# Projection pieces of 64 rows among the score tiles, and scores two units ahead, in an attention and expert kernel

## What is computed

```python
x = x + layernorm(attention(layernorm(x)))      # 16 heads of 16, biases on q, k, v and out
x = x + layernorm(experts(layernorm(x)))        # 16 experts of width 128, the best 8 mixed, and a shared one

# attention, per batch of 1024 tokens and per head:
scores = q @ k.T                                # q scaled by 1/4
attn = softmax(scores, axis=-1)
ctx = attn @ v
```

## Time and profile before

| | |
|---|---|
| median of 3 runs | 2850.79 us (2848.54 to 2851.70) |
| the profiled execution | 2851.26 us |
| its span, first to last instruction | 2849.5 us |
| mean granted clock of TensorE | 0.987 |
| PE busy | 96% of the span |
| DVE / ACT / POOL busy | 77% / 57% / 36% |
| attention stage, first to last product | 105.3 to 1644 us |

### The profile page before, as it was taken

The page is one execution under the profiler, slowest core; times in us unless marked ns, Lnnn a source line. Parts: engine busy times, 40 slices in busy tenths (PEclk is TensorE's granted clock), DMA queues, the critical chain, the costliest instruction groups (busy, mean ns, idle before and its releaser), DMA issues.

```text
span 2849.5 us, 47674 instructions
## 1 busy us (share of the span) xinstructions
PE 2738.6 (96%) x16514; PEld 1683.1 (59%) x16514; DVE 2207.1 (77%) x4585; ACT 1638.4 (57%) x3159; POOL 1039.5 (36%) x1057
## 2 busy tenths in 40 slices
PE   4999999999999999999999899999999999999997
PEld 2434333343343343433433388888888888888886
DVE  4898998999988989989899667666666666666654
ACT  1477777777777777877778843333333333333332
POOL 4042562654544635636545545111111111111112
PEclk8899999999999999999999999999999999999999
DMA  5303422343234144333332323222222222232221
GB/s 88 55 27 57 65 60 54 63 83 58 53 63 63 42 65 64 64 59 63 63 67 66 88 78 105 82 78 77 74 82 83 79 79 71 82 82 79 79 73 54
DMA packets 136640, 197.33 MB, mean 69 GB/s; under 512 B 22336, under 2 KB 84816, under 8 KB 134352
## 3 DMA queue, kind: packets, MB, share of 16 engines
q1 hardware_dynamic: 136400, 194.29, 31.0%
HBM read 108.74 MB, written 17.30 MB: 44 GB/s over the span
## 4 chain that ended last, share of the span: by engine, by line
PE 83%; SPq 7%; ACT 4%; DVE 3%; issue 2%; POOL 1%; DMA 1%; POOLq 0%; ACTq 0%; DVEq 0%
PE o_bank L558 15%; PE y_bank L681 13%; PE g_bank L667 13%; PE u_bank L667 13%; PE sm_bank L548 13%; PE st_bank L536 7%; SPq L340 4%; PE job_bank L582 4%; ACT probs L933 3%; PE job_bank L591 2%; DVE score_max L1044 1%; PE job_bank L603 1%; SPq L365 1%; SPq L364 1%; SPq L344 1%
## 5 line engine op out<-in xcount | busy, mean ns | idle before, releaser
L1044 DVE TENSOR_REDUCE score_max<-sm_bank 128x1 f32<-128x512 f32 x2048 | 1299.6, 681 | 140.7 <-PE sm_bank L548 136.5
L933 ACT ACTIVATE probs<-st_bank 128x512 f32<-128x512 f32 x2023 | 1080.5, 599 | 313.6 <-PE st_bank L536 310.7
L548 PE MATMUL sm_bank<-qk_stack 64*128 64x512 f32 x2048 | 794.2, 462 | 15.9 <-DMA qk_stack<-qk_stack 11.2
L536 PE MATMUL st_bank<-qk_stack 64*128 64x512 f32 x2023 | 750.0, 451 | 40.4 <-ACT probs L933 31.5
L548 PEld LDWEIGHTS sm_bank<-qk_stack 64*128 64x128 f32 x2048 | 331.6, 188 | 558.1 <-DVE score_max L1044 509.8
L558 PE MATMUL o_bank<-probs,v_quad 128*32 128x512 f32 x4096 | 547.9, 607 | 9.1 <-ACT o_sb L841 7.0
L1191 DVE TENSOR_TENSOR h<-gate_act,u_bank 128x512 f32<-128x512 f32 x256 | 176.2, 688 | 313.1 <-ACT gate_act L895 312.9
L895 ACT ACTIVATE gate_act<-g_bank 128x512 f32<-128x512 f32 x272 | 162.4, 597 | 418.3 <-PE u_bank L667 418.2
L536 PEld LDWEIGHTS st_bank<-qk_stack 64*128 64x128 f32 x2023 | 312.9, 185 | 123.6 <-ACT probs L933 97.3
L906 ACT ACTIVATE h_hi<-h 128x512 fp32r<-128x512 f32 x272 | 172.2, 633 | 325.0 <-DVE h L1194 287.2
L1474 POOL TENSOR_SCALAR f_x_in<-f_x_in,f_mv,f_rstd 128x256 f32<-128x256 f32 x64 | 90.5, 1424 | 616.8 <-DVE f_rstd L1105 616.8
(11 more groups left out here) (202 smaller groups left out, 3939.3 us busy)
## 6 DMA issues: line engine op xcount, KB each, us to landing
cb<-comb_dram SPq DMA_DIRECT2D x256, 256.0 KB, 3.7
qk_stack<-qk_parts SPq DMA_DIRECT2D x360, 128.0 KB
x_in<-in_x SPq DMA_DIRECT2D x8, 1024.0 KB, 6.0
o_part<-o_sb SPq DMA_DIRECT2D x256, 32.0 KB, 2.0
sum_part<-o_sb SPq DMA_DIRECT2D x256, 32.0 KB, 2.0
x_res<-in_x SPq DMA_DIRECT2D x16, 512.0 KB, 4.0
x<-x_res SPq DMA_DIRECT2D x16, 512.0 KB, 3.1
f_x_in<-x SPq DMA_DIRECT2D x16, 512.0 KB, 3.9
```

The costliest lines, as they stand in the source:

```text
L536: mm(bank_of(tile)[:, :], k_stack[q][p][rows, kc * CH:(kc + 1) * CH], q_stack[q][p][rows, f * HALF:(f + 1) * HALF], start=True, stop=True) ...
L548: mm(sm_bank[n % RING][:, :], q_stack[q][p][rows, tok:tok + CH], k_stack[q][p][rows, half * HALF:(half + 1) * HALF], start=True, stop=True ...
L933: nc.scalar.activation(probs[kc % 2][:, j, :], bank_of(4 * U + j)[:, :], ACT.Exp).then_inc(exp_done, 1)
L1044: v.reduce_max(score_max[f][:, HC * (2 * p + e) + c, half:half + 1], sm_bank[n % RING][:, :], AX_X).then_inc(smax_read, 1)
```

## The change

- The halves of XT, QK, V and OP are cut once more, by rows of the array: `job_rows` issues a third of a half (`third`) with 64 rows (`e`). A half of V or OP is now 12 matmuls of 64x256, one of QK 6 of 64x512, and a transposition job 8 transposes of 64 rows instead of 4. They stand among the score tiles and the maxima of the other row half. Between e = 0 and e = 1 PE waits for its own semaphore `job_rows_done`.
- `st` is called for the unit after the next: the tiles 4U + 8 to 4U + 11 stand in unit U, all behind the product. The heads go in the order `HEAD_AT`, the maxima in the order `MAX_AT`.
- `JOBS` has other units: the two halves of a job are neighbours, and SH, XT, QK and V move by some units.
- ACT reads a job's bank two of its units later, ahead of its last Exp; the splits and four other steps of ACT move by one unit.
- On SP `gather(b, 4)` and `load_shift(b, 6)` go ahead of `load_stack(b + 1, 0)`.

```diff
+HEAD_AT = (1, 3, 0, 2)
+
+MAX_AT = {True: ((0, 1), (1, 1), (0, 0), (1, 0)), False: ((0, 0), (1, 0), (0, 1), (1, 1))}
...
-JOBS = {
-    23: ("XT", 1, 0, None), 24: ("XT", 1, 1, None), 27: ("XT", 1, 2, None), 28: ("XT", 1, 3, None),
-}
-for _s in range(STEPS):
-    JOBS[8 * _s + 1] = ("SH", 0, _s + 1, None)
+JOBS = {}
+for _i, _u in enumerate((1, 9, 17, 25, 32, 41, 49, 57)):
+    JOBS[_u] = ("SH", 0, _i + 1, None)
+for _i, _u in enumerate((22, 24, 26, 28)):
+    JOBS[_u] = ("XT", 1, _i, None)
 for _kind, _off, _i, _at in (
-        ("OP", -1, 0, (5, 6, 7, 8)), ("OP", -1, 2, (15, 16, 20, 21)),
-        ("QK", 1, 0, (29, 30, 31, 32, 35, 36, 37, 38)), ("V", 1, 0, (39, 40, 43, 44, 45, 46, 47, 48)),
-        ("QK", 1, 4, (51, 52, 53, 54, 55, 56, 59, 60))):
+        ("OP", -1, 0, (5, 7)), ("OP", -1, 2, (15, 20)), ("QK", 1, 0, (30, 33, 36, 39)),
+        ("V", 1, 0, (42, 44, 47, 50)), ("QK", 1, 4, (52, 55, 58, 61))):
     for _n, _u in enumerate(_at):
-        JOBS[_u] = (_kind, _off, _i + _n // 2, _n % 2)
+        for _part in range(2):
+            JOBS[_u + _part] = (_kind, _off, _i + _n, _part)
...
+def among_scores(u, first, last):
+
+    return u in JOBS and JOBS[u][0] != "SH" and not skipped(JOBS[u], first, last)
...
+                gather(b, 4)
+                load_shift(b, 6)
                 if not last:
                     load_stack(b + 1, 0, False)
-                gather(b, 4)
-                load_shift(b, 6)
                 if not first:
                     store_x1(b - 1, 1)
...
-            def st(U, s, kc, j, new_step):
-
-                q, f, p, e, tile = s // 2, s % 2, j // 2, j % 2, 4 * U + j
-                if new_step is not None:
-                    pe.wait_ge(shift_loaded, 64 * (new_step + 1))
+            def st(tile):
+
+                U, i = tile // 4, tile % 4
+                if U >= UNITS * BATCHES:
+                    return
+                S, kc, j = U // CHUNKS, U % CHUNKS, HEAD_AT[i]
+                s = S % STEPS
+                q, f, p, e = s // 2, s % 2, j // 2, j % 2
+                if kc == 0 and i == 0:
+                    pe.wait_ge(shift_loaded, 64 * (S + 1))
...
+            def job_rows(job, b, e, third):
+
+
+                kind, off, i, part = job
+                B = b + off
+                rows = slice(64 * e, 64 * e + 64)
+                if third == 0:
+                    if e == 1 or part == 1:
+                        pe.wait_ge(job_rows_done, rows_done[0])
+                    if e == 0 and part != 1:
+                        if before:
+                            pe.wait_ge(*before.pop(0))
+                        before.append((job_read[kind], nth(kind, B, i)))
...
+                if kind == "XT":
+                    half, k = i // 2, i % 2
+                    for c in ((0, 1), (2,), (3,))[third]:
+                        at = c * CH + 64 * e
+                        last = nc.tensor.transpose(job_bank[:, at:at + 64],
+                                                   x_in[rows, half * HC + c, k * 128:(k + 1) * 128], ident[rows, rows])
+                elif kind == "QK":
+                    m, half, n = i // 4, i // 2 % 2, "qk"[i % 2]
+                    a, w = PARTS[third]
+                    last = mm(job_bank[:, :], w_parts[n][w][rows, part, m * 128:(m + 1) * 128],
+                              xT[a][rows, part, half * HALF:(half + 1) * HALF],
+                              start=(part == 0 and third == 0 and e == 0), stop=(part == 1 and third == 2 and e == 1))
+                else:
...
+                    for k in range(KD):
+                        last = mm(job_bank[:, part * D:(part + 1) * D], left[a][rows, k, c * CH:(c + 1) * CH],
+                                  right[w][rows, k, :], start=(e == 0 and third == 0 and k == 0),
+                                  stop=(e == 1 and third == 2 and k == KD - 1))
+                if third == 2:
+                    if e == 1 and part != 0:
+                        last.then_inc(job_ready[kind], 1)
+                    else:
+                        last.then_inc(job_rows_done, 1)
+                        rows_done[0] += 1
...
-            for j in range(RING):
-                st(0, 0, 0, j, 0)
+            for tile in range(8):
+                st(tile)
...
+                    if with_job:
+
+                        maximum(0)
+                        job_rows(JOBS[u], b, 0, 0)
+                        st(4 * U + 8)
+                        job_rows(JOBS[u], b, 0, 1)
+                        maximum(1)
+                        job_rows(JOBS[u], b, 0, 2)
+                        maximum(2)
+                        st(4 * U + 9)
+                        st(4 * U + 10)
+                        job_rows(JOBS[u], b, 1, 0)
+                        maximum(3)
+                        job_rows(JOBS[u], b, 1, 1)
+                        st(4 * U + 11)
+                        job_rows(JOBS[u], b, 1, 2)
+                    else:
+                        st(4 * U + 8)
+                        maximum(0)
+                        st(4 * U + 9)
+                        maximum(1)
+                        maximum(2)
+                        st(4 * U + 10)
+                        if u in JOBS and not skipped(JOBS[u], first, last):
+                            job("SH", b, JOBS[u][2])
+                        maximum(3)
+                        st(4 * U + 11)
...
                     for j in range(4):
+                        if j == 3 and U >= 2:
+
+                            at, of = (u - 2, b) if u >= 2 else (u - 2 + UNITS, b - 1)
+                            if at in JOBS and not skipped(JOBS[at], of == 0, of == BATCHES - 1):
+                                kind, off, i, part = JOBS[at]
+                                if part != 0:
+                                    job(kind, of + off, i)
                         act.wait_ge(st_ready, 4 * U + j + 1)
...
-                        nc.scalar.activation(probs[kc % 2][:, j, :], bank_of(4 * U + j)[:, :],
+                        nc.scalar.activation(probs[kc % 2][:, HEAD_AT[j], :], bank_of(4 * U + j)[:, :],
...
-                    if u in SPLITS and not (first and SPLITS[u][0]):
-                        off, f, k = SPLITS[u]
+                    if u - 1 in SPLITS and not (first and SPLITS[u - 1][0]):
+                        off, f, k = SPLITS[u - 1]
                         split_hi(b + off, f, k)
```

More of the change, by code:

```diff
@@ L214, in both_stages @@
         pv_done = sem("pv_done")
+        job_rows_done = sem("job_rows_done")
         smax_ready = sem("smax_ready")
@@ L537, in st, with smax @@
                    q_stack[q][p][rows, f * HALF:(f + 1) * HALF], start=True, stop=True).then_inc(st_ready, 1)
-            def smax(S, s, kc, half, e):
+            def smax(S, s, kc, i, with_job):
                 q, f = s // 2, s % 2
                 p, c = kc // HC, kc % HC
+                half, e = MAX_AT[with_job][i]
                 tok = f * HALF + c * CH
-                n = 32 * S + 4 * kc + 2 * half + e
+                n = 32 * S + 4 * kc + i
                 if n >= RING:
@@ L553, in pv @@
                 q = s // 2
-                if kc == 0 and not (isinstance(S, int) and S == 0):
+                if kc == 0 and S > 0:
                     pe.wait_ge(o_stored, S)
@@ L720, in batch, with maximum @@
                         pe.wait_ge(v_copied, QUADS * b + s // 2 + 1)
-                    def maximum(half, e):
+                    with_job = among_scores(u, first, last)
+                    def maximum(i):
                         if maxima:
[L724 to L740, removed]
+                            smax(S + 2, (s + 2) % STEPS, kc, i, with_job)
                     if last and u == UNITS - 1:
@@ L743, in batch @@
                     pv(U, S, s, kc)
[L744 to L752, removed]
-                    maximum(1, 1)
+                    if with_job:
[13 more added lines that the diff above has]
+                        job_rows(JOBS[u], b, 1, 2)
+                    else:
+                        st(4 * U + 8)
[8 more added lines that the diff above has]
+                        st(4 * U + 11)
                     if last:
@@ L936, in batch @@
                         store_o(S)
-                    if u - 1 in JOBS and not skipped(JOBS[u - 1], first, last):
-                        kind, off, i, part = JOBS[u - 1]
-                        if part != 0:
-                            job(kind, b + off, i)
-                    if u in SPLITS and not (first and SPLITS[u][0]):
-                        off, f, k = SPLITS[u]
+                    if u - 1 in SPLITS and not (first and SPLITS[u - 1][0]):
+                        off, f, k = SPLITS[u - 1]
                         split_hi(b + off, f, k)
@@ L953, in batch @@
                             squares(0, u - 32)
[L954 to L958 removed]
+                        if u in (47, 49):
+                            gT_hi((u - 47) // 2)
+                        if u in (52, 54):
```

(14 more changed lines are left out.)

23 lines of the change are left out of this document (14 added, 9 removed).

## The result

The changed kernel takes 2881.66 us (median of 4 runs, 2874.1 to 2882.94) against 2851.24 for the kernel before in the same session (4 runs, 2848.54 to 2854.23): 1.0101 times as long, 95% interval 1.0081 to 1.0121. It is slower by 1.0%. 2847 was forecast, with the sign the other way. The time is near the upper end of the whole range, which reaches to the 2885 of the pieces that gain nothing, and above the 2838 to 2858 that I gave to my own account. The profiled execution took 2881.35 us.

A forecast was written before the change was run, and what follows sets the result against it. Plain units were bound by a three-bank ring through three engines, job units by TensorE. Batches 1 to 6 stayed at 194.2 us; batches 0 and 7 made 2851.3 - 3.9 = 2847.4, so 2847; range 2820 to 2885, own account 2838 to 2858.

The forecast's parts named there:

- the pieces that gain nothing: Rival: the wait between halves eats what pairing saves, units with half a job stay at 3.22 us; 2885 us, chance 0.12.
- the sum: Adding the stretches of a batch of 1 to 6, waits and clock included: 194.2 us, as before the change.
- the term that TensorE bounds: From the shift's landing at unit 14 to product 35: 1.7 + 12 x 2.92 + 8 x 2.73 = 58.6 us.
- the queue's stretch: From product 35 to the landing of step 7's shift, at the end of SP's row of issues: 62.2 us.
- the clock: Half clock after waits of TensorE: 1.6 us lost after unit 14, 0.8 after unit 54, 2.4 a batch.
- the tail: From the landing of step 7's shift to the batch's end: 1.7 + 6 x 2.92 + 3 x 2.73 = 27.5 us.
- the landing: Step 2's shift, wanted at unit 14, lands 43.5 us after the batch's start; wanted at 40.0, a wait of 3.5.
- batches 0 and 7: First and last batch, counted apart: batch 0 at 187.6 us against 189.9, batch 7 shorter by 1.6.
- the rival with slots of 0.34: Rival: each 512-column slot on TensorE takes 0.34 us, a job unit 3.55; 2939 us in all, chance 0.08.
- plain units leave 2.70: Sign that the forecast is wrong: units without a piece of a job no longer take about 2.70 us.
- 28 at 2.73: The 28 plain units of a batch at 2.73 us; with 36 at 2.92, 181.6 us if nothing else ended later.
- waits cost less: Rival: the clock stays up through the waits, 2831 us, or 2820 with landings 1 us earlier; chance 0.20.

The follow-up runs named there:

- the kernel with 5 transfers: The changed kernel with load_stack cut to 5 of its 14 transfers, so the stacks hold one head in four: 2798.08 us.
- the best kernel: The changed kernel with load_stack(b, 3) behind load_shift(b, 2), the first split earlier, and load_shift(b, 7) ahead of gather(b, 5): 2802.12 us.
- both edits of the queue: load_stack(b, 3) moved behind load_shift(b, 2), and the first split earlier on ACT and POOL: 2821.96 us on the changed kernel, 2843.4 on the kernel before.
- the shifts first alone: The changed kernel with only load_shift(b, 2) ahead of gather(b, 0) and load_shift(b, 7) ahead of gather(b, 5): 2837.05 us.

## Why the prediction was wrong

The mechanism forecast is the one that ran: shorter units, and a queue of SP that hands the gain back. The step that failed is **the sum**. It let gain and loss of a batch cancel to the tenth, 194.2 before and after, so its sign hung on small errors in the terms, and all five terms came out too small. The largest miss is the term that TensorE bounds, from unit 16 to product 35: it took 55.8 us where 54.0 were counted, because a plain unit behind a pair of QK pieces was priced like any other. Then come the queue's stretch (63.3 for 62.2), the clock (0.7), the tail (0.4) and the landing (0.3): 4.3 us a batch, to which batches 0 and 7 add 9.1 in all, and the kernel is 1.0% slower instead of the same. That the rival in which the pieces gain nothing gave 2885, close to the time measured, is chance: its unit of 3.22 us did not occur.

**Right: the units with a piece.** 2.92 was forecast, 2.94 to 2.97 measured. Four slots are the forecast 0.23, but a fifth, near the end, is 0.34, so TensorE's own sum is 2.95 and not 2.81; and the fourth tile of maxima starts 2.27 us after the product, not 2.35. The two errors nearly cancel, and why the late slot is longer was not tried. The rival with slots of 0.34 fell, and so did the one in which the pieces gain nothing: with the queue out of the way they bring 7.1 us a batch. Rows agree that weight loads of the two halves do not take turns: in the timeline of weight loads of the same unit (kernel after) a tile of each half loads at once.

```profile
618.44 0.18 PEld L564 LDWEIGHTS sm_bank<-qk_stack 64*128 64x128 f32 x1 [0.84 <-DVE score_max L1119]
618.44 0.18 PEld L658 LDWEIGHTS job_bank<-xT_hi,wk_hi 64*128 64x128 f32 x1
618.54 0.19 PEld L551 LDWEIGHTS st_bank<-qk_stack 64*128 64x128 f32 x1
618.55 0.19 PEld L658 LDWEIGHTS job_bank<-xT_lo,wk_hi 64*128 64x128 f32 x1
```

By the Trainium skill, "TensorEngine Tiling (Array Packing)", Key Properties, different tiles load and multiply in parallel; this trace agrees (618.44 twice).

**Right: the queue of SP takes the gain.** Segment by segment, as means over batches 1 to 6: the shift lands at 43.75 us from the batch's start (43.5 forecast). From product 35, `ctx_split` comes after 19.4 (2.73 + 16.5) and the shift of step 7 after 63.3 (62.2). The two places of waiting are the forecast ones. The idle time was less than the forecast 30 to 40 us for the shift and 15 to 25 for the stack (24.5 and 11.5 over six batches) because the units ahead of it were longer; this is no gain. The sign "plain units leave 2.70" came true in part: in the kernel with 5 transfers 18 of 28 stand at 2.73 to 2.78, and three at 3.15 to 4.51.

**Wrong, first: the term "28 at 2.73" and its sum 181.6.** In the kernel without the waits (5 transfers), the medians of the units with a piece add up to 106.9 us (36 at 2.97; 105.1 forecast) and those of the plain units to 81.1 (28 at 2.90; 76.4 forecast): 6.4 more. The largest part, 2.8, is two plain units: 41 at 4.51 and 32 at 3.72. Both hold the transposition for the shift right behind a pair of QK pieces, so that PE waits for VectorE's read of `job_bank`, 5.2 us in 12 times in the waits above, and for banks of maxima that VectorE reads late in the same unit (0.50 and 0.32 us in the timeline above). VectorE has the reads of maxima, the maxima's combination and, in unit 41, the seeds ahead of the read. I had counted jobs by TensorE's work alone and had not followed the neighbour of a job in the new table. In the stretch between unit 16 and product 35, which TensorE bounds, unit 32's 1.0 us and smaller ones made 55.8 us of 54.0. In the one from product 35 on, SP's queue sets the time (1.1 us off its forecast), so what unit 41 took longer only shortened the wait behind it.

**Wrong, second: the clock at "1.6 + 0.8".** From the landing of the shift at unit 14 to product 16 it took 6.97 us on average; the kernels without that wait take 4.77, where 4.6 was counted, so the half clock cost 2.2 and not 1.6. It was 6.8 us long in five of the six batches, as in the window above, where the earlier trace rows had 3.4. After unit 41 or 48 it fell in every one of them. That made unit 48 3.98 us long and not 2.97, but as forecast it only ate into the wait behind it; the tail behind the shift of step 7 took 28.7 us, for 27.5 + 0.8. Here the clock was overpriced: it fell after unit 54 in one batch of six, not in half, and the best kernel, without a fall, has a tail of 28.4, so it is the 27.5 that was short.

**Wrong, third: batch 0 and batch 7.** Batch 0 took 193.6 us, not 187.6. Its first two units took 4.20 and 3.47 at half clock, and unit 47, with the wait for the stack, took 7.91. Batch 7, from its first product to its last, went from 182.1 to 183.6, where 1.6 less was forecast: 3.1 more.

The account by measured terms: 4.3 x 6 (198.5 against 194.2) + 6.0 + 3.1 = 34.9 over the forecast 2847.4, which is 2882.3 against 2881.35. The 4.3 itself: 0.3 for the landing, 0.7 clock and 1.8 units to product 35, 1.1 in the queue's stretch, 0.4 behind it.

**Where the change's expected gain went.** On the kernel before, both edits of the queue give 2843.4; with table, readers, scores two ahead and the changed order of SP as well, but whole jobs, 2852.6; with pieces and the shift of step 7 ahead of its gather, 2802.1. So the pieces bring 50 us, the rest costs 9 (the first halves in units 5, 15, 33, 36 and 39 take 3.43 to 3.46 us, not 3.22; why was not tried), and the changed queue, with the clock that falls behind its waits, takes all but 3.5 of the 50. The rival "waits cost less" fell: in the changed kernel the clock fell in every batch.

## What to carry to other kernels

When units of an engine get shorter, hold every transfer whose issue chain does not get shorter against the new time at which it is wanted: here 1.0% slower became 1.7% faster by moving two steps of SP's queue and one split of ACT and POOL. Place small, urgent transfers (a 2.6 us shift) ahead of long ones that are wanted later (a 5.2 us gather, a 12.9 us stack). After an edit of a job table, look at what stands right behind each moved job on its engine and which other engine must have read its bank; and before moving a small step to get it out of the way, follow who waits for it on every queue.

## What the hardware showed that was not expected

- **A tiny VectorE instruction took as long as POOL's beside it.** L1100 works on 128x4 elements. In the kernel after it started at 620.74, beside POOL's L1519 (620.66 to 621.94), and ended at 621.97 (timelines above). Groups by form of the kernel after and of the one with both edits (busy us, mean ns):

```profile
L1100 DVE TENSOR_SCALAR rstd_a<-rstd_a 128x4 int32<-128x4 int32 x16 | 10.1, 629 | 0.5
```

```profile
L1101 DVE TENSOR_SCALAR rstd_a<-rstd_a 128x4 int32<-128x4 int32 x16 | 2.8, 172 | 0.5
```

  The 629 ns is a mean of seven at 1.14 to 1.23 us, each beside L1519 and ending 0.03 us behind it, and nine at 0.17 to 0.20. With the split moved away from beside it, the mean fell to 172 ns and unit 41 from 4.51 to 3.29 us. Not every instruction of POOL does this: one L1100, at 1751.45 us, took 0.20 beside L1533, which ran on for 0.95. By the Trainium skill, "Advanced Engine Details and Errata", Mode Summary, VectorE's second port is shared with GpSimd, and GpSimd's instructions and those of VectorE's two-port modes block each other. The rows beside L1519 agree in the length, the one beside L1533 does not, and none shows the port.
- **The clock fell without a wait for a transfer.** In the kernel with the shifts first alone, it was at the 1.2 GHz level for 3.4 us behind unit 41 of batch 2, a unit with three waits for VectorE of 0.16 to 0.49 us. In the kernel with 5 transfers it fell twice in batches 1 to 6, both times where unit 41 ends (from 405.4 and 784.3 us). In the best kernel, where unit 41 takes 3.30 us, it did not fall in batches 1 to 7.
- **Stretches at half clock were 3.4 us long or 6.8** in batches 1 to 6 of every kernel. The length of the wait does not tell which: at unit 14 of the changed kernel it was 3.4 behind 3.77 us (batch 3) and 6.8 behind 2.24 us (batch 5).
